# Turning half 1's tiles by DVE blocks and two HBM scratch tensors instead of 16 TensorE transposes

## The reference

```python
x = x + _L0_xattn_ref(_layernorm(x, axis=-1), ids, ctx, ctx, ctx)
x = x + _L0_ffn_ref(_layernorm(x, axis=-1), router_w, e_bias, gate_up_proj, down_proj, ...)
```

## Time and profile before

| | before |
|---|---|
| median of 3 runs | 173.74 us (173.63 to 174.43) |
| profiled execution, its own time | 173.89 us |
| span in its trace, first to last instruction | 171.8 us |
| PE busy / DVE busy / ACT busy / POOL busy | 166.6 / 114.2 / 67.8 / 39.6 us |
| chain that ended last | PE 97% of the span |
| granted TensorE clock, mean | 1.000 of full speed |

### The profile page before, as it was taken

How to read it: one execution, slowest core, us unless ns; L and a number is a source line. 1 busy time by engine, 2 the same in 40 slices (tenths; PEclk the granted TensorE clock), 3 DMA queues, 4 the chain that set the end, 5 groups by cost and what they waited for, 6 DMA issues and landing times.

```text
span 171.8 us, 2194 instructions
## 1 busy us (share of the span) xinstructions
PE 166.6 (97%) x728; PEld 130.6 (76%) x728; DVE 114.2 (66%) x230; ACT 67.8 (39%) x112; POOL 39.6 (23%) x37
## 2 busy tenths in 40 slices
PE   6989999999999999999999999999999999999992
PEld 2568888888877888788787778788787887878881
DVE  0779778888984988588688528964744444444452
ACT  2472520551258254824664593152212222223320
POOL 2593000698200025539385000000000000000000
PEclk9999999999999999999999999999999999999999
DMA  4999000176400036742111200043361211100003
GB/s 137 307 373 352 23 4 2 25 236 227 122 0 4 15 130 181 203 160 67 61 61 61 61 0 4 8 126 126 113 195 45 75 65 61 62 0 4 2 0 122
DMA packets 7971, 16.41 MB, mean 95 GB/s; under 512 B 1336, under 2 KB 2200, under 8 KB 7832
## 3 DMA queue, kind: packets, MB, share of 16 engines
q1 hardware_dynamic: 7960, 16.27, 29.0%
HBM read 15.08 MB, written 1.18 MB: 95 GB/s over the span
## 4 chain that ended last, share of the span: by engine, by line
PE 97%; ACT 0%; POOL 0%; DVE 0%; issue 0%; DVEq 0%; POOLq 0%
PE bank L853 26%; PE bank L913 14%; PE bank L911 13%; PE bank L912 13%; PE bank L931 7%; PE bank L934 7%; PE bank L932 7%; PE bank L943 4%; PE bank L820 2%; PE bank L907 1%; PE bank L908 1%; PE bank L832 1%; ACT xn_hi L433 0%; POOL warm L383 0%; DVE xt L732 0%
## 5 line engine op out<-in xcount | busy, mean ns | idle before, releaser
L913 PE MATMUL bank<-xn_lo,gu_hi 128*128 128x512 f32 (+1 forms) x104 | 41.0, 394 | 0.0
L911 PE MATMUL bank<-xn_hi,gu_lo 128*128 128x512 f32 x96 | 37.9, 395 | 0.0
L912 PE MATMUL bank<-xn_hi,gu_hi 128*128 128x512 f32 x96 | 37.8, 394 | 0.0
L501 ACT ACTIVATE h_hi<-hid 128x512 fp32r<-128x512 f32 (+1 forms) x26 | 16.4, 632 | 45.7 <-DVE hid L720 45.7
L725 DVE TENSOR_TENSOR h_lo<-hid,h_hi 128x512 fp32r<-128x512 f32 (+1 forms) x26 | 20.2, 778 | 15.6 <-ACT h_hi L501 15.6
L913 PEld LDWEIGHTS bank<-xn_lo,gu_hi 128*128 128x128 f32 (+1 forms) x104 | 19.4, 186 | 5.0
L491 ACT ACTIVATE act_sb<-bank 128x512 f32<-128x512 f32 (+1 forms) x26 | 15.4, 594 | 18.1 <-PE bank L913 18.0
L398 POOL TENSOR_TENSOR gu_lo<-stage,gu_hi 128x512 fp32r<-128x512 f32 x12 | 17.9, 1516 | 17.6 <-ACT gu_hi L426 17.6
L912 PEld LDWEIGHTS bank<-xn_hi,gu_hi 128*128 128x128 f32 x96 | 18.0, 187 | 4.4
L911 PEld LDWEIGHTS bank<-xn_hi,gu_lo 128*128 128x128 f32 x96 | 18.0, 187 | 4.4
L931 PE MATMUL bank<-h_hi,wd_lo 128*128 128x512 f32 (+1 forms) x52 | 20.6, 396 | 0.0
(11 more groups left out here) (76 smaller groups left out, 213.1 us busy)
## 6 DMA issues: line engine op xcount, KB each, us to landing
stage<-gu_d SPq DMA_DIRECT2D x6, 512.0 KB, 3.5
stage<-wd_d SPq DMA_DIRECT2D x3, 512.0 KB, 4.1
x<-comb_d SPq DMA_DIRECT2D x8, 192.0 KB, 2.7
ids<-comb_d SPq DMA_DIRECT2D x8, 192.0 KB, 3.0
stage<-ctx_d SPq DMA_DIRECT2D x4, 256.0 KB, 5.0
xt<-xt_d SPq DMA_DIRECT2D x1, 1024.0 KB, 10.3
x<-comb_d SPq DMA_DIRECT2D x8, 128.0 KB, 3.1
ids<-comb_d SPq DMA_DIRECT2D x8, 128.0 KB, 2.8
```

The source lines that it names most:

```text
L911: nc.tensor.matmul(out[:], gu_lo[:, cols], xn_hi[:, h, k], start=(k == 0), stop=False)
L912: nc.tensor.matmul(out[:], gu_hi[:, cols], xn_hi[:, h, k], start=False, stop=False)
L913: ins = nc.tensor.matmul(out[0:rows, :], gu_hi[:, wide], xn_lo[:, h, k], start=False, stop=(k == KC - 1))
```

## The change

TensorE no longer turns anything for half 1. DVE turns x1 in 32x32 blocks (`turn_x1`, two instructions, behind place 1), SP writes the blocks to the HBM tensor `x1_d` in four DMAs (ahead of place 6's spread) and reads them back in four (ahead of place 8's spread), so that tokens stand on partitions. The statistics move from behind place 3 to behind place 5, the applying from behind place 5 to behind place 6. DVE then turns the normalised tiles in blocks (`turn_xn`, four instructions, ahead of place 7's product), SP writes them to `xn_d` and reads them back into `xn`, seen as `xn_turn`, with features on partitions. `copy_x1` goes. With `early = 10` half 1's shared chunk stands at place 11; half 0's chunks 9 and 10 come ahead of it; places 12 to 25 hold the same items as before. The scores are normalised one place behind the shared chunk (place 12), before two places behind it (place 11). POOL's code is untouched.

```diff
-X1_AT = 2
+QUARTERS = P // LANES
+X1_TURN, X1_WRITE, X1_READ, X1_STATS, X1_APPLY = 1, 5, 7, 5, 6
+XN_TURN, XN_WRITE, XN_READ = 7, 11, 12
...
-        early = 8
+        early = 10
...
+            def write_x1():
+                sp.wait_ge(x1_turned, KC)
+                rows = x1_d.rearrange("(b j) (q c) -> q j b c", j=LANES, q=QUARTERS)
+                blocks = x[:, TT:].rearrange("p t d -> p (t d)").rearrange("p (b c) -> p b c", c=KC * LANES)
+                for q in range(QUARTERS):
+                    sp.dma_start(rows[q], blocks[q * LANES:(q + 1) * LANES]).then_inc(x1_out, 16)
+
+            def read_x1():
+                sp.wait_ge(x1_out, QUARTERS * 16)
+                rows = x1_d.rearrange("(b t j) f -> b j t f", t=TT, j=LANES)
+                for b in range(QUARTERS):
+                    sp.dma_start(x[b * LANES:(b + 1) * LANES, TT:], rows[b]).then_inc(x1_back, 16)
+
+            def write_xn():
+                sp.wait_ge(xn_turned, TT)
+                rows = xn_d.rearrange("q k i (b c) -> b i (q k) c", c=P)
+                blocks = x[:, TT:].rearrange("p t d -> p (t d)").rearrange("p (m c) -> p m c", c=P)
+                for b in range(QUARTERS):
+                    sp.dma_start(rows[b], blocks[b * LANES:(b + 1) * LANES]).then_inc(xn_out, 16)
+
+            def read_xn():
+                sp.wait_ge(xn_out, QUARTERS * 16)
+                for k in range(KC):
+                    sp.dma_start(xn_turn[:, k], xn_d[:, k]).then_inc(xn_back, 16)
...
-            def copy_x1(h):
...
             def tile_stats(n, t):
                 if n > HALVES:
-                    dve.wait_ge(x1_copied, t // (TT // KC) + 1)
+                    dve.wait_ge(x1_back, QUARTERS * 16)
...
+            def turn_x1():
+
+                dve.wait_ge(x1_done, HALVES * KC)
+                dve.wait_ge(normed_a, HALVES * TT // 2)
+                for k in range(KC):
+                    nc.vector.transpose(x1_blocks[:, k], xt[:, k, HALF:].rearrange("p (b j) -> p b j", j=LANES)).then_inc(x1_turned, 1)
+
+            def turn_xn():
+
+                dve.wait_ge(normed_a, NORMS * TT // 2)
+                dve.wait_ge(normed_v, NORMS * TT // 2)
+                for t in range(TT):
+                    nc.vector.transpose(xn_blocks[:, t], xn[:, t].rearrange("p (m i) -> p m i", i=LANES)).then_inc(xn_turned, 1)
...
-                if g == place[1, 0] + 2:
+                if g == place[1, 0] + 1:
                     normalise_scores(1, mark_best(1))
```

More of the change, by code:

```diff
@@ L130, in build @@
         comb_row = sb("comb_row", [P, HALVES, P])
+        x1_blocks = x[:, TT:].rearrange("p t d -> p (t d)").rearrange("p (b k i) -> p k b i", k=KC, i=LANES)
+        xn_blocks = x[:, TT:].rearrange("p t d -> p (t d)").rearrange("p (m t i) -> p t m i", t=TT, i=LANES)
+        xn_turn = xn[:].rearrange("p t d -> p (t d)").rearrange("p (k c) -> p k c", k=KC)
+        x1_d = nc.dram_tensor("x1_d", (HALF, D), F32, kind="Internal").ap()
+        xn_d = nc.dram_tensor("xn_d", (QUARTERS, KC, LANES, HALF), F32, kind="Internal").ap()
         comb_d = nc.dram_tensor("comb_d", (HALVES, LANES, HALF), F32, kind="Internal").ap()
@@ L147, in build @@
         rows_out, rows_turned = [sem(f"rows_out{h}") for h in range(HALVES)], sem("rows_turned")
-        comb_zero, x1_copied = sem("comb_zero"), sem("x1_copied")
+        comb_zero = sem("comb_zero")
+        x1_turned, x1_out, x1_back = sem("x1_turned"), sem("x1_out"), sem("x1_back")
+        xn_turned, xn_out, xn_back = sem("xn_turned"), sem("xn_out"), sem("xn_back")
         dstep = sem("dstep")
@@ L171, in build @@
                       ("x1", 0, 0, 4), ("x1", 0, 1, 5), ("n2", 0, 0, 4), ("n2", 0, 1, 5)]
[L172 to L176, removed]
         side_at = {u[:3]: n for n, u in enumerate(side_order)}
@@ L214, in side_bank, with features, wait_features @@
             return bank[side_order[side_at[what, h, c]][3]]
+        def features(what, h, k):
+            return xn_turn[:, k] if (what, h) == ("n2", 1) else side_bank(what, h, k)[:]
+        def wait_features(eng, what, h, k):
+            if (what, h) == ("n2", 1):
+                eng.wait_ge(xn_back, KC * 16)
+            else:
+                eng.wait_ge(side_done, side_at[what, h, k] + 1)
         def widths(c):
@@ L375, in _ @@
                     load_piece(len(pieces) - 2 + (g == 6))
+                if g == X1_WRITE:
+                    write_x1()
+                if g == X1_READ:
+                    read_x1()
+                if g == XN_WRITE:
+                    write_xn()
+                if g == XN_READ:
+                    read_xn()
                 if g == place[1, SPREADS]:
@@ L428, in x_high @@
             def x_high(what, h, k):
-                act.wait_ge(side_done, side_at[what, h, k] + 1)
+                wait_features(act, what, h, k)
                 if what == "n2":
                     act.wait_ge(z_done, (mixed[1, h, KC - 1] + 1) * E1)
-                nc.scalar.activation(xn_hi[:, h, k], side_bank(what, h, k)[:], ACT.Copy).then_inc(xhi_done, 1)
+                nc.scalar.activation(xn_hi[:, h, k], features(what, h, k), ACT.Copy).then_inc(xhi_done, 1)
             def first_z(n):
@@ L600, in x_low @@
                 dve.wait_ge(xhi_done, n + 1)
-                dve.wait_ge(side_done, side_at[what, h, k] + 1)
-                nc.vector.tensor_tensor(xn_lo[:, h, k], side_bank(what, h, k)[:], xn_hi[:, h, k].bitcast(F32),
+                wait_features(dve, what, h, k)
+                nc.vector.tensor_tensor(xn_lo[:, h, k], features(what, h, k), xn_hi[:, h, k].bitcast(F32),
                                         ALU.subtract).then_inc(xlo_done, 1)
@@ L787, in _ @@
                     x_low("n2", 1, 1)
+                if g == XN_TURN:
+                    turn_xn()
                 product(g)
@@ L796, in _ @@
                 hid_low(g)
-                if g == 3:
+                if g == X1_TURN:
+                    turn_x1()
+                if g == X1_STATS:
                     for t in range(TT):
```

15 lines of the change are left out of this document (3 added, 12 removed).

## The result

The changed kernel took 180.56 us (median of 4, 180.28 to 180.88) against 173.88 for the kernel before (median of 4): ratio 1.038, 95% interval 1.0345 to 1.0415. The forecast was 177.1 with a range of 175.0 to 179.0: right in sign and in both waits that it named, too low in size.

A forecast was written before the change was run, and what follows sets the result against it. TensorE, busy 166.6 of 171.8 us, was taken as the bound. Terms of -1.75, +3.25 and +1.9 us summed to +3.4 on the median of 173.74, giving 177.1 us, with a range of 175.0 to 179.0.

The forecast's parts named there:

- The removed transposes: On TensorE, two groups of 8 transposes for half 1 go, 0.88 us a group: -1.75 us.
- The added DVE work at no cost: DVE's block turns, 1.4 us behind place 1 and about 1.6 ahead of product(7), are absorbed; up to 3 us without cover.
- First new wait: At place 7 TensorE waits 3.25 us (bounds 2.5 to 3.8) for weight piece 11, behind POOL's power and the later statistics.
- Second new wait: In place 16 TensorE waits 1.9 us (bounds 0.9 to 2.7) for output(0), through half 1's rows and product(14).
- The xn trip at no cost: xn's HBM round trip, read back on 4 engines, lands near 100.5, ahead of place 11, with about 1 us left.
- The granted clock: At place 7's wait the clock might fall, each us at the lower level costing 0.5; left out of the sum.
- The x1 trip at no cost: x1's HBM round trip lands at 78 to 80, before DVE asks behind h_lo(5) at 80.9; 1 to 3 us in hand.
- Only piece 11 is late: Rival: half 1's rows land 1.9 us sooner than half 0's, so output(0) is in time; 175.2 us, chance 0.13.
- faster: Rival: POOL does a power and a piece in 3.2 us, so neither wait occurs; 172.0 us, chance 0.07.
- a third delay: Rival: late x1, late xn or a lower clock at place 7 adds 1 to 3 us; 178.1 to 180, chance 0.17.

The follow-up runs named there:

- best version: Changed kernel with POOL's power behind pieces 11 and 12, pieces 13 and 14 after the applied norm, first downs in place 17, xn read in quarters: 171.90 us.
- the kernel with the 2.35 us: Changed kernel with POOL's power behind piece 11 and xn read back in four quarters, half 1's first downs still in place 16: 175.95 us, ratio 1.0114.

## Why the forecast was right in sign and wrong in size

**The removed transposes, -1.75.** Right. The best version, in which nothing waits, gains 2.0 us in the medians and 1.9 in the spans (169.9), which is 0.1 to 0.3 more than the 1.75; where that small rest comes from stays open.

**The added DVE work at no cost.** Right in the changed kernel, where place 7's wait covers for it. Without that cover TensorE waits 0.56 to 0.59 us at place 9 for DVE's `hid` of place 7, in the runs with the power moved. The four turns alone are not the reason: in the best version they still take 1.42 us and nothing waits.

**First new wait, 3.25 us forecast.** Right: 3.14, released by POOL's piece 11, and shown by moving either side of it (the power back, or the statistics alone).

**Second new wait, 1.9 us forecast.** Right in place and releaser, small in size: 2.30 with 0.10 of restart. The forecast had set the scoring chain without a late xn. xn was back at 103.4, not at 100.5, and the rows were turned 9.1 us behind the start of place 12, not 8.7; with xn read in quarters the wait was 1.47 us, and with the shared chunk moved alone 1.42, both inside the bounds that were given (0.9 to 2.7).

**The xn trip at no cost.** This step failed, if not by much here: the late xn is 0.8 us of the second wait. That the read gets 4 engines was forecast, but it took 8.7 us from issue to landing, not 7.0; and it was not forecast that DVE's shift and applies would take 3.95 us in place of 0.88 with POOL at work. The prediction saw product and POOL slow each other, and charged it only inside the bounds of the first wait. TensorE did not wait for xn, because place 7's wait and its slow matmuls gave it 4.7 us; the run with the power moved shows the price without that cover, 4.26 us at place 11 and 2.2 of slow matmuls.

**The granted clock.** This is the step that put the time out of the range. The prediction's sum, -1.75 + 3.25 + 1.9, has no term for it: it added the waits as if they cost only their length, and kept the slower clock for a rival of 0.17 together with two other delays. Measured, each of the two waits cost about 1.55 us more in slow matmuls, 3.1 in all, most of 180.56 - 177.1 = 3.5. The rest is the second wait's 0.5, less 0.1 of the first. The rule of the Trainium skill that was cited there (TensorE: Matmul & The Clock Gate, HAM oscillation) names waits of some us between matmuls as what brings the slower clock. It pointed this way, and the trace agrees with it: granted clock 0.50 for 3.2 us behind a wait of 3.14.

**The x1 trip at no cost.** Right in the profiled execution, by luck: DVE did not wait, but x1 was there less than 0.1 us ahead of it, not 1 to 3. The four reads took 4.9 to 5.6 us from issue to landing where the forecast had taken 2.7; they ran beside weight loads and spreads. In two of the runs, with the same trip, DVE waited 0.28 and 0.62 us for x1. The writes in 256-byte runs took 2.9 us from issue to landing against 2.3 for the 512-byte ones of xn, the same 128 KB each. They had other traffic beside them, so what the short runs cost is not shown.

**The rivals.** "Only piece 11 is late" and "faster" fell with the trace. Of "a third delay" the clock came true and the late xn half: it moved the second wait. Its 178.1 to 180 was still too low for both waits with their slow matmuls.

## What to carry to other kernels

Where TensorE is the bound and never waits, look for what else shares the queue of the moved step, and ask what that neighbour is due for: here a power of 1.4 us carried a weight piece past its place. Do not count a wait of TensorE at its length alone: those of 2.3 to 3.2 us here mostly cost another 1.5 us or so in slow matmuls, though not in every execution. And mend such waits together, since each covers for the next: moving the power alone gained 0.7 us of 4.7, and all mends together 8.7.

## What the runs showed of the hardware

In the profiled executions, waits of TensorE of 1.26, 1.27, 1.42 and 1.47 us were followed by no matmul at half clock; those of 2.30, 2.35, 3.14, 3.15 and 4.26 us each by eight to eleven. Behind 2.30 us, and in the run with the quarters alone behind 3.14, the slow ones began only with the sixth matmul. Why there and not at once stays open, and so does why the kernel with the 2.35 us met them in only two of its four executions.

DVE's shift (0.15 us by itself) took 1.22 us beside POOL's subtractions, and its two applies (0.73 together) 2.73; the four block turns took 1.42 us in the changed kernel and in the best version, both times beside POOL. The Trainium skill (SBUF — State Buffer, Who interferes with whom) says that a DVE instruction with two SBUF inputs, or a `tensor_scalar` in a mode that takes both port pairs, shares a pair with GpSimd, and that whichever comes second waits for the other's whole instruction. The shift has two SBUF inputs and the applies are `tensor_scalar`; by that rule, the trace agrees for the shift, which is 1.07 us longer, less than one POOL instruction of 1.3 to 1.5. The applies are about 1.0 us longer each, but no row shows in which mode they run: alone, one of 128x256 takes 0.41 us, as long as a block turn of that size (0.40). That it is POOL, by whatever way, is shown by the last run, in which it stands still at that time.
